# Thirteen pairs by seven products and one made plainly, in place of twelve pairs and twice 512 plain columns

## The reference, cut to what matters

```
x = x + attn(layernorm(x))      # one token per row here, softmax over one score: attn returns its input twice over
x = x + ffn(layernorm(x), weight, bias, kk, aa)

def ffn(x, weight, bias, kk, aa):
    w_b = aa * jnp.tanh(kk * weight)            # weight: 4096 x 4096
    y = jnp.einsum('bsi,oi->bso', x, w_b)
    return y + bias
```

## Time and profile before

| what | value |
|---|---|
| three runs | 472.76 us median (472.45 to 551.07) |
| the profiled execution | 471.84 us |
| its span, slowest core (core 1) | 470.3 us |
| spans of the eight cores | 462.9 to 470.3 us |
| PE busy | 434.6 us (92%) |
| DVE, ACT, POOL busy | 320.8, 193.8, 203.8 us |
| matmuls of 512 columns in L735 and L755 | 512 and 1344 |

### The profile page before, as it was taken

The page is one execution under the profiler, slowest core; times in us unless marked ns, Lnnn a source line. Parts: engine busy times, 40 slices in busy tenths (PEclk is TensorE's granted clock), DMA queues, the critical chain, the costliest instruction groups (busy, mean ns, idle before and its releaser), DMA issues.

```text
span 470.3 us, 7035 instructions; the slowest of 8 cores (462.9 to 470.3 us)
## 1 busy us (share of the span) xinstructions
PE 434.6 (92%) x2184; PEld 206.2 (44%) x2184; DVE 320.8 (68%) x474; ACT 193.8 (41%) x181; POOL 203.8 (43%) x188
## 2 busy tenths in 40 slices
PE   0656789999999999989999999999999999999997
PEld 0634345544444444434444444444444444444443
DVE  2788687487642899999675858675656666667552
ACT  0478767637933414124424243424333333333000
POOL 0222112122530861397637464647473838386300
PEclk9857998999999999999999999999999999999999
DMA  7999999974999759659997959795959696957101
GB/s 172 313 288 319 302 348 298 288 224 147 295 276 315 263 195 293 211 156 289 302 325 231 343 166 312 235 305 195 324 180 325 201 319 212 329 168 284 57 31 60
DMA packets 36612, 116.37 MB, mean 247 GB/s; under 512 B 5088, under 2 KB 5088, under 8 KB 36576
## 3 DMA queue, kind: packets, MB, share of 16 engines
q1 hardware_dynamic: 23472, 84.43, 56.6%
q0 software_dynamic: 5760, 18.88, 14.0%
q10 hardware_dynamic: 7344, 12.62, 7.2%
HBM read 99.14 MB, written 16.78 MB: 246 GB/s over the span
## 4 chain that ended last, share of the span: by engine, by line
PE 64%; DMA 16%; DVE 6%; DVEq 5%; ACT 3%; issue 3%; SPq 2%; ACTq 0%
PE acc L755 55%; DMA wr<-wpieces 12%; PE acc L735 7%; DMA early<-x 4%; DVEq L479 3%; PE acc L706 2%; SPq L289 1%; ACT late L618 1%; DVEq L520 1%; DVEq L532 1%; ACT early L626 1%; DVE early L524 1%; DVE late L503 1%; DVE h2T L503 1%; SPq L295 0%
## 5 line engine op out<-in xcount | busy, mean ns | idle before, releaser
L676 ACT ACTIVATE late<-wr,kk_sb 128x1024 bf16<-128x1024 f32 x48 | 53.3, 1143 | 96.1 <-PE acc L755 41.8
L676 ACT ACTIVATE early<-wr,kk_sb 128x1024 bf16<-128x1024 f32 x48 | 53.4, 1143 | 87.6 <-PE acc L755 44.6
L755 PE MATMUL acc<-h2T,late 128*128 128x512 bf16 x384 | 85.0, 379 | 1.4 <-DVE late L524 1.4
L755 PE MATMUL acc<-h2T,early 128*128 128x512 bf16 x384 | 84.8, 379 | 0.0
L735 PE MATMUL acc<-early,h2T 128*128 128x512 bf16 x256 | 62.4, 395 | 3.3 <-ACT early L618 3.3
L755 PEld LDWEIGHTS acc<-h2T,late 128*128 128x128 bf16 x384 | 37.5, 98 | 47.0 <-issue 1.8
L755 PEld LDWEIGHTS acc<-h2T,early 128*128 128x128 bf16 x384 | 37.6, 98 | 45.3
L735 PE MATMUL acc<-late,h2T 128*128 128x512 bf16 x256 | 57.0, 379 | 0.0
L537 DVE SCALAR_TENSOR_TENSOR early<-acc,early 128x512 f32<-128x512 f32 x48 | 33.2, 692 | 33.0 <-PE acc L755 26.8
L537 DVE SCALAR_TENSOR_TENSOR late<-acc,late 128x512 f32<-128x512 f32 x48 | 33.2, 692 | 31.9 <-PE acc L755 28.8
L368 POOL TENSOR_TENSOR early<-early 128x512 f32<-128x512 f32 x24 | 34.6, 1440 | 40.4 <-DMA early<-xt 29.5
(11 more groups left out here) (58 smaller groups left out, 428.4 us busy)
## 6 DMA issues: line engine op xcount, KB each, us to landing
wr<-wpieces SPq DMA_DIRECT2D x128, 512.0 KB, 7.9
early<-x SPq DMA_DIRECT2D x24, 512.0 KB, 13.8
early<-xt POOLq DMA_DIRECT2D x24, 256.0 KB, 6.9
late<-xt POOLq DMA_DIRECT2D x24, 256.0 KB, 6.3
yt<-early ACTq DMA_DIRECT2D x24, 256.0 KB, 5.0
yt<-late ACTq DMA_DIRECT2D x24, 256.0 KB, 6.3
h2T<-x SPq DMA_DIRECT2D x8, 512.0 KB, 19.9
y<-late POOLq DMA_DIRECT2D x16, 256.0 KB, 7.0
```

The source lines that it names most:

```text
L676: scalar.activation(slot[b, j % 2][:, k * PW:(k + 1) * PW], wr[w % RING][:, :], AF.Tanh, bias=0.0, scale=kk[:, :]).then_inc(s_wt, 1)
L755: mm = tensor.matmul(acc[pbank[j, m]][:, :], slot[b, j % 2][:, k * 128:(k + 1) * 128], a[:, :, k * 128:(k + 1) * 128], start=(k == 0), sto ...
```

## The change

Only 512 outputs stay plain; the other 3584 are fourteen pairs. The first pair (pair 0) isn't made by seven products but plainly, in four groups of 32 matmuls for its four quarters (unit "G", token half, output half, eighth; 8 matmuls each, L727 of the new kernel). Its groups stand around T6 and T7 as filler, where the second 512 plain columns stood. The first pair by seven products is pair 1. The second load of residuals is gone, `xt` for pairs 0 and 1 is asked for right after T7, and the first half of pair 1's residuals overwrites stored plain results. VectorE makes sA5 before the first evictions, and sA2, the M7 operand and sA1 before the sums of pair 1's weights; the M6 operand is made once group G(1, 0) is done. Only then come the takes of pair 0 (`take_first`), and M6, M7, M1 of pair 1 and M5 of pair 2 use the banks that these free.

```
-NO = 2
+NO = 1
-TANH_BEFORE = [1, 4, 7, 10, 13, 16, 20, 26]
+TANH_BEFORE = [1, 4, 7, 10, 13, 16, 20, 23]
-EARLY = 5
+FIRST = [(0, 1), (0, 0), (1, 1), (1, 0)]
...
     products(5)
-    for p in range(3):
-        todo += second(p)
-    join(6, [], second(3))
+    todo += [("G", 0, 1, 0), ("G", 0, 1, 1), ("G", 0, 1, 2)]
+    todo += [("T", 6, 0), ("T", 6, 1), ("G", 0, 1, 3), ("T", 6, 2), ("T", 6, 3)]
     products(6)
-    for p in range(4, 6):
-        todo += second(p)
-    join(7, [], second(6))
+    todo += [("G", 0, 0, 4)]
+    todo += [("T", 7, 0), ("T", 7, 1), ("G", 0, 0, 5), ("T", 7, 2), ("G", 0, 0, 6), ("T", 7, 3)]
     products(7)
...
+    todo.insert(len(todo) - 9, ("G", 0, 0, 7))
+    todo.insert(len(todo) - 6, ("R", 0))
+    todo += [("G", 1, 1, 0), ("R", 1), ("G", 1, 1, 1), ("G", 1, 1, 2), ("G", 1, 1, 3)]
+    todo += [("G", 1, 0, p) for p in range(4, 8)]
...
+        elif last:
+            free.append((bank_of[g], ("rd", FIRST.index(g[1:]) + 1)))
+    pool = [(6, ("rc", 4)), (7, ("rc", 4))] + sorted(free, key=lambda v: v[1][0] != "ev")
+    order_of = [FIRST] + [PRODUCTS] * (NP - 2) + [LAST_PRODUCTS]
...
+        for j in range(2):                       # GpSimd
+            for q in QUARTERS:
+                load_xt(j, q)
+        for i in range(NT - 2, NT):
+            serve(i)
         gpsimd.wait_ge(s_rc, 4)
+        gpsimd.wait_ge(s_sa, 4)
+        for j in range(2):
+            for q in QUARTERS:
+                residual(j, q)
...
             if t == 6:                           # VectorE
+                wait_transposed(vector, 3, NCH - 1)
+                add_tiles(tiles(sA5), quarter(0, 0), quarter(0, 1), ALU.add)
                 for i in range(5):
                     evict(i)
...
         spread()
+        evict(6)
+        wait_transposed(vector, 7, NCH - 1)
+        add_tiles(tiles(sA2), quarter(1, 0), quarter(1, 1), ALU.add)
+        vector.wait_ge(s_mm, nth_product[0, (0, 0)])
+        add_tiles(quarter(0, 1), quarter(0, 1), quarter(1, 1), ALU.subtract)
         evict(7)
+        add_tiles(tiles(sA1), quarter(0, 0), quarter(1, 1), ALU.add)
+        sums(1, ["S6", "D12"])
+        sums(1, ["S7", "D21"])
+        vector.wait_ge(s_mm, nth_product[0, (1, 0)])
+        add_tiles(quarter(1, 0), quarter(1, 0), quarter(0, 0), ALU.subtract)
+        sums(1, ["S1"])
+        for q in FIRST:
+            take_first(q)
...
+        while w < W0 + 8:                        # ScalarE
+            tanh_piece(w)
+            w += 1
         copy_rows(0)
+        scalar.wait_ge(s_grp, NT)
```

More of the change, by code:

```diff
@@ L147, in build_nc @@
     h2b = part(early, 32, 8)
-    wp = [part(early, 40, 32), part(late, 0, 32)]
+    wp = part(early, 40, 32)
     base = [part(late, 32 + 2 * t, 2, F32) for t in range(NT)]
-    bb = [part(late, 48 + 2 * i, 2, F32) for i in range(2)]
-    sA5, sA2, sA1 = part(early, 0, 16), part(early, 16, 16), part(late, 0, 16)
+    bb = part(late, 48, 2, F32)
+    sA5, sA2, sA1 = part(late, 0, 16), part(early, 0, 16), part(early, 56, 16)
     CT = [[part(early, 32 + 4 * o, 4, F32) for o in range(2)], [part(late, 32 + 4 * o, 4, F32) for o in range(2)]]
@@ L191, in build_nc @@
     s_base = sem("s_base")
-    s_b0 = [sem(f"s_b0{i}") for i in range(2)]
+    s_b0 = sem("s_b0")
     s_nD = sem("s_nD")
@@ L339, in serve @@
                              base[t][:, :]).then_inc(s_y[t], 16)
[L341 to L344, removed]
         for t in range(NT):
             normalize(t)
-        for i in range(NT - 1):
+        for i in range(NT - 2):
             serve(i)
@@ L650, in copy_rows @@
         def copy_rows(half):
+            if half == 0:
+                scalar.wait_ge(s_base, NT)
             for i in range(2):
@@ L723, in _ @@
                 continue
+            if u[0] == "G":
+                _, i, o, p = u
+                if W0 + p >= seen_w:
+                    seen_w = W0 + p + 1
+                    tensor.wait_ge(s_wt, seen_w)
+                wait_transposed(tensor, 4 * i + 3, NCH - 1)
+                if p % 4 == 0:
+                    kind, n = bank_free["G", i, o]
+                    tensor.wait_ge({"ev": s_ev, "rd": s_rd}[kind], n)
+                b = BLOCKS[p // 2]
+                a = quarter(i, int(b[1]) - 1)
+                for k in range(8 * (p % 2), 8 * (p % 2) + 8):
+                    mm = tensor.matmul(acc[bank_of["G", i, o]][:, :], slot[b, 0][:, k * 128:(k + 1) * 128],
+                                       a[:, :, k * 128:(k + 1) * 128],
+                                       start=(p % 4 == 0 and k == 0), stop=(p % 4 == 3 and k == 15))
+                if p % 4 == 3:
+                    mm.then_inc(s_mm, 1)
+                continue
             _, t, ot, p = u
@@ L740, in _ @@
                 mm.then_inc(s_grp, 1)
-        for j in range(NP):
+        for j in range(1, NP):
             for m in order_of[j]:
```

204 lines of the change are left out of this document (77 added, 127 removed).

## The result

The changed kernel takes 476.43 us in the median of four runs (475.43 to 477.87), the kernel before 472.61 on the same chip: a ratio of 1.0092 [1.0066, 1.0118], slower by 0.9%. So the sign was wrong. That 476.43 still lies inside the stated range of 466.5 to 476.5 is luck: it does so by 0.07 us, and two of the four runs lie above it. The profiled execution took 476.98 us, with a span of 475.4 on its slowest core.

What follows compares the result with a forecast made beforehand. PE, busy 92%, was taken as the bound, so only matmul count and PE's waits count. -3.5 + 1.3 - 1.0 - 1.9 + 3.0 + 1.3 = -0.8 gave 471.0 profiled, 472 us median; range 466.5 to 476.5, the forecast's own 470 to 475.

Steps and rivals of the forecast that it cites:

- the sign: Whole kernel: slightly faster, -0.8 us against the profiled execution's 471.84.
- the sum's single wait: PE at M6 of pair 1: waits +3 us for DVE's take of pair 0, bounds 0 and 5.
- A second wait, in pair 2: Rival, 12%: pair 2's residuals come late, so PE waits 3 to 6 us more at M1: 475 to 478 us.
- Fewer matmuls: PE overall: 1840 matmuls instead of 1856, sixteen fewer at 0.216 us, -3.5 us.
- T6: Tile 6's transposes: input no sooner but six filler matmuls missing, so PE stands +1.3 us; sA5 costs nothing.
- T7: Tile 7's transposes: the wait of 1.01 us goes, with three tanh pieces ahead instead of six, -1.0 us.
- The passage to products: From T7 to pair 1's first product: it begins at 146.6, and waits of 0.55 and 1.38 go, -1.9 us.
- M6's wait and its mechanism: M6 of pair 1: DVE's nine additions alternate with POOL's residuals at 2.25 us each, delaying pair 0's take; +3 us.
- The clock: Behind M6's wait: PE runs at a lower clock after idling, +1.3 us, bounds 0 and 1.9.
- DVE isn't late: Rival, 30%: M6 of pair 1 waits for nothing and the clock stays, -5.1 us, which is 467.7.

Runs made afterwards that it cites:

- Loads: Changed kernel with all four loads of pair 2's xt issued at once and M5's two quarters made first: 472.56 us, ratio 0.9967; again on another chip 0.9992.
- small residuals: Changed kernel with the residuals of pairs 0 and 1 computed on one column of 512, output not right: 472.05 us, ratio 0.9954.
- the repeated run: The changed kernel measured again without an edit, on another occasion: 478.09 us, ratio 1.0074.
- the runs with T6 moved: T6 and T7 one group of eight matmuls later: on the changed kernel 1.0081, with loads and take edits 1.0012, with loads, take and sums edits 0.9945.
- POOL sooner: Kernel of "Loads", with POOL starting pair 0's residuals without waiting for DVE's sA1: 474.72 us, ratio 1.0054.
- Loads, take, sums: Changed kernel with pair 2's loads at once, two pair 0 takes before pair 1's S1, and pair 2's S7, D21 right behind S6, D12: 468.27 us, 0.9944.
- take alone: Changed kernel with DVE taking the first two quarters of pair 0 before S1 of pair 1: 477.65 us, ratio 1.0066.

## Why the prediction was wrong, step by step

**The step that failed** is the sum's single wait. It put +3.0 for M6 of pair 1, and for all later ones nothing ("One more pair has its 12 takes and 5 sums under 24.2 us of PE, as the others"). The prediction had the other case as its second rival, "A second wait, in pair 2", with the mechanism as it came out: residuals of pair 2 late, DVE's take waiting, S1 behind it, M1 of pair 2 idle, 475 to 478 us. It gave this 12%. By its own numbers it was nearer than that: with the residual at 190, two steps of the take (1.5) and S1 (1.2) end at 192.7, already behind the 191.5 at which M1 needs S1, and only M6's wait ahead of it left a margin. And the residual came at 194.4 on core 6. POOL began pair 2's loads at 171.64 and issued them in two rounds; the rows [11] show 3.73 and 3.19 us of waiting for a load where loads are issued early, while in a round with nothing ahead the whole time from issue to landing counts: 7.34 and 7.14 us here. The runs showed in its place two more waits on the slowest core, 2.47 and 2.21 us, and 1.6 by the clock behind the second. "Loads" removes these waits and brings the time down by 1.1%; "small residuals" shows that without the turns of pairs 0 and 1 they remain on half of the cores.

**Against core 6 the miss adds up.** Forecast 471.0 for the profiled execution, measured 476.98, 6.0 more. The first product begins at 149.01 and not 146.6: 2.4, of which 1.6 are the clock at T6 and 0.7 that T6 begins at 104.86 and not 104.12. The waits behind it sum to 6.37 and not 3.0: 3.4. The clock 1.6 and not 1.3: 0.3. That is 6.1.

**Fewer matmuls**, right: 2168 instructions on PE and not 2184, at 0.216 us a matmul.

**T6**, mis-sized. Forecast +1.3, measured 2.01 in the mean of the cores. The prediction gave the addition sA5 4.62 us under 5.88 of idle; it took 5.46, because POOL's normalization ran beside it, and the first eviction followed at 88.73 with no idle left. From there T6 is as far as before: 104.12 - 87.98 = 16.1 then, 104.86 - 88.73 = 16.1 now. Where DVE had idle time left behind sA5 (core 3 of the repeated run, 0.81 us), T6's wait was 1.45, the forecast's 1.3 and the 0.15 of before. The clock lost behind this wait wasn't in the sum at all. But the runs with T6 moved show that neither mattered for the end: without them the wait at M6 would have been longer.

**T7**, right: no wait (118.73 on core 6). **The passage to products**, right in its length: 44.15 us from T6 to the first product, of which 1.6 are clock, against 42.5 forecast; core 1 began at 147.07.

**M6's wait and its mechanism**, right. On core 6 the four additions of h2T tiles take 8.91, the first take releases M6, the wait is 1.69; over the cores it is 0.15 to 2.7, inside the bounds of 0 to 5, with a mean of 1.25 under the 3.0 taken. "Small residuals" and "POOL sooner" show the turns as its cause from both sides.
The Trainium skill ("SBUF — State Buffer", "Who interferes with whom") has the two exclude each other for a whole instruction. The rows agree in kind; the price by that rule, 2.5 for an addition, is more than the 8.91 / 4 = 2.23 measured.

**The clock**, mis-sized by place. On core 6 T6's wait and the last one cost 1.6 each, and M6's 1.69 cost nothing; the sum had put 1.3 behind M6.

**"DVE isn't late"** (30%, 467.7) did not happen on core 6. "Loads, take, sums", which has no such wait, has a median of 468.27 and looks like the 467.7, but ran on a faster chip: its gain is 0.56%, some 2.6 us, about half of the 5.1 of the sum without late waits. T6 takes 0.7 more than forecast there; for the rest no run here gives the terms.

**One core for eight.** The sum held on core 1 of one execution to the tenth, by chance and by errors that partly cancel (T6 began 1.4 us sooner than forecast and cost 1.8 by the clock), but the metric is the slowest core's. Before the change the late waits were 0.55 and 1.38 us on it, and core 6 had a single one of 1.24. After it, the sum of the four later columns ran from 2.2 to 6.4 over cores that run the same program. In part that follows the landings: the three cores that wait at M1 of pair 2 (2, 6 and 7) are among the four whose second round waited longest, 3.44, 4.68 and 4.44 us. In part it follows what PE had lost before, and the turns, as on cores 1 and 0 above. In the repeated run the slowest core was again the one with the slowest landings. So a chain with DMA round trips in it should be costed with slow landings as well, since the metric takes the worst of eight cores.

What stays open: why loads land later on some cores than on others, and on others again in the next run; how much of the wait for D21 of pair 3 is the rounds and how much the turns; and whether another order of the M6 operand on DVE would let T6's 2 us be won, which wasn't tried.

## What to carry to other kernels

When a change shortens TensorE's road to a new stage, follow the helper engines' chain (store, load, residual, take, weight sum) through its second round and not only to the first wait, and price each round by issue to landing, on the slowest core. Waits in a row are not independent terms: taking out the first (take, T6) gave nothing while the chain behind it was late, and mending that chain (loads) exposed the next one in DVE's written order (sums). T6's wait gave nothing even then. Test the cures together: take alone changed the ratio from 1.0074 to 1.0066, loads alone to 0.9967 and 0.9992, and the three edits together to 0.9944.

## What the hardware showed unexpectedly

Two idle times of PE of the same length can differ in price. On core 6 the 2.01 us at T6 was followed by a granted clock of 0.55 and cost 1.6 us, and the 2.21 at M4 of pair 3 by 0.52; after 2.47 us at M1 of pair 2, the longest of the four, sixteen matmuls took 3.61, the full pace. It is so from core to core as well: behind the same 2.0 us at T6 the first eight matmuls of pair 0 took 1.89 us on cores 2 and 7 and 2.88 to 3.54 on the other six. Nothing that was read here tells the two kinds apart.

DVE's bf16 additions go in turns not only with POOL's residuals (2.23 us each and not 1.16) but once with its normalization as well: four took 5.46 and not 4.62 ahead of T6. There it is POOL that pays most, 7.06 us for two normalized chunks that take 2.94 without DVE's additions (core 6, at 82.41 and 103.45). A longer stretch of such company costs both engines: on core 6 POOL's residual instructions went from 1.27 to between 2.06 and 2.26 each while DVE added.
